# A fused loop over sequences: a written-out order for its head and its first two periods

## What is computed

```
h = silu(t @ sw1.T) * (t @ sw3.T)                  # shared expert of the first mixture
gate, xBC, dt = split(x @ W_in)
x, B, C = split(silu(conv4(xBC) + conv_b))
dt = softplus(dt + dt_bias); dA = exp(-exp(A_log) * dt)
h_t = h_(t-1) * dA_t + (dt_t * x_t) B_t;  y_t = h_t C_t + D_skip * x_t
y = rmsnorm(y * silu(gate)) * norm_w;     out = y @ W_out
w = top8(sigmoid(h @ gate_w)) normalised * 2.5     # second mixture
moe = shared(h) + sum_e w_e * (silu(h @ Wg_e) * (h @ Wu_e)) @ Wd_e
```

## Time and profile before

| | us |
|---|---|
| median of 3 runs | 1946.59 |
| lowest, highest | 1942.2, 1947.4 |
| the profiled execution | 1942.54 |
| its span (first to last instruction) | 1940.8 |
| TensorE busy | 1824.9 (94%) |
| VectorE busy | 1296.4 (67%) |
| ScalarE busy | 752.2 (39%) |
| GpSimd busy | 425.2 (22%) |
| mean granted clock of TensorE | 0.965 |

### The profile page before, as it was taken

How to read it: one execution, slowest core, us unless ns; L and a number is a source line. 1 busy time by engine, 2 the same in 40 slices (tenths; PEclk the granted TensorE clock), 3 DMA queues, 4 the chain that set the end, 5 groups by cost and what they waited for, 6 DMA issues and landing times.

```text
span 1940.8 us, 33575 instructions
## 1 busy us (share of the span) xinstructions
PE 1824.9 (94%) x9916; PEld 1406.5 (72%) x9917; DVE 1296.4 (67%) x3768; ACT 752.2 (39%) x1451; POOL 425.2 (22%) x708
## 2 busy tenths in 40 slices
...
DMA packets 92136, 137.88 MB, mean 71 GB/s; under 512 B 18564, under 2 KB 76164, under 8 KB 91524
## 3 DMA queue, kind: packets, MB, share of 16 engines
...
## 4 chain that ended last, share of the span: by engine, by line
PE 40%; issue 39%; DVE 11%; POOL 7%; ACT 2%; DMA 1%; DVEq 0%; POOLq 0%; SPq 0%; ACTq 0%
PE bank L610 6%; PE bank L184 5%; PE bank L631 4%; PE bank L1316 3%; POOL sorted_in L858 3%; PE bank L1274 2%; PE bank L193 2%; PE bank L1379 2%; PE bank L1322 2%; PE bank L1304 2%; PE bank L1407 2%; DVE tops L1560 1%; PE bank L621 1%; PE bank L539 1%; POOL down_w L2202 1%
## 5 line engine op out<-in xcount | busy, mean ns | idle before, releaser
L184 PE MATMUL bank<-moe_xT,up_w 128*128 128x256 f32 x2304 | 547.9, 381 | 0.0
L184 PEld LDWEIGHTS bank<-moe_xT,up_w 128*128 128x128 f32 x2304 | 439.8, 191 | 60.5 <-issue 0.2
L227 ACT ACTIVATE moe_silu<-bank 128x256 f32<-128x256 f32 x288 | 110.7, 384 | 574.6 <-PE bank L184 574.6
L193 PE MATMUL bank<-down_w,moe_hT 128*128 128x256 f32 x1152 | 304.0, 387 | 3.5 <-ACT moe_y L230 2.1
L193 PEld LDWEIGHTS bank<-down_w,moe_hT 128*128 128x128 f32 x1152 | 207.1, 190 | 37.0 <-issue 6.3
L1560 DVE TENSOR_REDUCE tops<-bank 128x4 f32<-128x1024 f32 (+1 forms) x96 | 117.4, 1223 | 54.7 <-PE bank L1316 52.9
L1461 ACT ACTIVATE probs<-bank 128x1024 f32<-128x1024 f32 x96 | 98.4, 1025 | 117.2 <-PE bank L1322 117.2
L830 DVE TENSOR_TENSOR moe_h<-moe_silu,bank 128x176 f32<-128x176 f32 x80 | 27.0, 338 | 138.7 <-issue 86.0
L610 PE MATMUL bank<-up_w,moe_xT 128*128 x320 | 115.5, 484 | 0.9 <-ACT moe_xT L676 0.6
L1316 PE MATMUL bank<-kT,qT 16*128 16x256 f32 (+1 forms) x1024 | 114.1, 351 | 0.0
L294 DVE TENSOR_TENSOR moe_hT<-moe_silu,bank 128x256 f32<-128x256 f32 x256 | 107.6, 420 | 8.8
...
...
## 6 DMA issues: line engine op xcount, KB each, us to landing
...
up_w<-in_up SPq DMA_DIRECT2D x2, 2304.0 KB, 12.6
```

Source lines behind the costliest of these rows:

```text
L184: last = mm(k.bank[:, UP_BANK + i % 3, half * S:(half + 1) * S], m.w_up[:, c, at + half * m.inter:at + (half + 1) * m.inter], m.xT[:, par, ...
L193: last = mm(k.bank[:, SUM_BANK, j * D:(j + 1) * D], m.hT[:, i % 3, j * P:(j + 1) * P], m.w_down[:, m.expert(i), :], start=(i == 0 and j == ...
L227: nc.scalar.activation(m.silu[:, i % 3, :], k.bank[:, UP_BANK + i % 3, 0:S], ACT.Silu).then_inc(m.silu_ready, 1)
```

## The change

- The order of the head is another one: the three `l_up` of `b` stand together behind `turn_dt` of sequence 0, and their silus are steps of their own (`l_silu`), behind the decay's transpose. `turn_dA`, `decay_out` and `decay_in` of sequence 0 stand ahead of its gates.
- Period 0 is the written-out list `FIRST`. The softplus and the decay of sequence 1 follow its `gating` 1 directly, its gates and convolution come behind, and `c_sum`, `c_norm`, `norm` and `turn_x` of sequence 2 are gone from it. At its end it has `up` 0 to 2, `h` 0 and 1 and `down` 0 of sequence 0, and `gmat` of sequence 1 ahead of `turn_c` of sequence 1.
- Period 1 is the written-out table `SECOND`, with 15 rounds (n = 3 to 17). The sum and norm of sequence 2 stand between the scans of sequence 1, the projections of sequence 2 two to four rounds later than before, and the sum and norm of sequence 3 at the end. Its rounds have `h` behind the other steps.
- The four products of `w_out` with `norm_w` on VectorE move from the start of the fused loop to the first mixture, ahead of its blocks.
- Waits of `m_turn`, `m_turn_c`, `turn_x` and `turn_c` are changed for the first sequences, to fit the bank's new order.

```diff
@@ moe_tensor
-            if not isinstance(t, int) or t + 1 < SEQS:
+            if isinstance(t, int) and t == 0:
+                pe.wait_ge(ssm.gate_ready, 4)
+            elif not isinstance(t, int) or t + 1 < SEQS:
                 pe.wait_ge(ssm.xtok_ready, 2 * t + 4)
...
-            if not isinstance(t, int) or t + 2 < SEQS:
+            if not isinstance(t, int) or 0 < t and t + 2 < SEQS:
                 pe.wait_ge(ssm.xT_ready, t + 3)
@@ sparse_vector
+    scale_w_out(k, m.ssm, dve)
     seen = [0]
@@ late_scalar
-        if what == "l_up":
+        if what == "l_silu":
@@ ssm_tensor
-            if begun(t - 1):
+            if isinstance(t, int) and t in (1, 2):
+                pe.wait_ge(m.xtok_ready, 2 * t)
+            elif begun(t - 1):
                 pe.wait_ge(moe.exp_ready, t - 1)
-            elif t == 1:
-                pe.wait_ge(m.xtok_ready, 2)
...
                 pe.wait_ge(m.gate_ready, 2 * t + 2)
+                if isinstance(t, int) and t == 1:
+                    pe.wait_ge(moe.combT_ready, 1)
@@
+def scale_w_out(k, m, dve):
+    dve.wait_ge(m.loaded, m.LOADS)
+    for f in range(FT):
+        last = k.nc.vector.tensor_scalar(m.w_out[:, f, :], m.w_out[:, f, :], m.norm_w[:, f:f + 1], None, ALU.mult)
+    last.then_inc(m.w_out_ready, 1)
@@ Tail
+    FIRST = (
+        ("gmat", 0, 0), ("scan", 0, 0), ("weight", 0, 0), ("c_fetch", 2, 0),
...
+        ("up", 0, 2), ("h", 0, 1), ("down", 0, 0), ("gmat", 1, 0), ("turn_c", 1, 0), ("turn_c", 1, 1),
+    )
+    SECOND = (
+        (("scan", 1, 0), ("weight", 1, 0), ("c_sum", 2, 0), ("xdt", 1, 0)),
...
+    )
@@ head
-        yield from self.period(0, 0)
-        yield "l_end", B, 0, 0
-        yield from self.period(1, 1)
+        for what, t, i in self.FIRST:
+            yield what, t, t % 2, i
+        for n, then in enumerate(self.SECOND, 3):
+            for what, t, i in (("up", 0, n), *then, ("h", 0, n - 1), ("down", 0, n - self.LAG)):
+                yield what, t, t % 2, i
```

More of the change, by code:

```diff
@@ L903, in sparse_sync @@
     go_through(m.blocks, sp, block)
-LATE_STEPS = ("l_norm", "l_turn", "l_up", "l_h", "l_down", "l_end")
+LATE_STEPS = ("l_norm", "l_turn", "l_up", "l_silu", "l_h", "l_down", "l_end")
 class Late:
```

44 lines of the change are left out of this document (33 added, 11 removed).

## The result

The changed kernel took 1952.49 us (median of 6 runs, 1949.52 to 1958.66) against 1946.25 before (6 runs) on the same chip in turns: a ratio of 1.0034, 95% interval 1.0019 to 1.005. It is slower by some 6 us. The forecast was 1947.0, which is 0.4 over the median then known, with a range of 1934.5 to 1957.0. The time is in the range, on the slow side, and 5.5 over the forecast.

What follows compares the result with a forecast made beforehand. Bound: TensorE in the hardware loop, before it a chain through VectorE, ScalarE and TensorE. First `up` +0.6 plus 1.9 for the clock gave +2.5: 1945.0 on the profiled execution, 1949.1 on the median, set at 1947; range 1934.5 to 1957.

Steps and rivals of the forecast that it cites:

- The start: Start of the fused loop: the four `w_out` products leave it and cost nothing in the first mixture, -1.2 us.
- The head: Steps up to `gating` 0: `turn_dt` spared two `l_up` (1.7), less waits; with a shorter decay DMA wait, -1.45 us in all.
- Period 0: Stretch from `gating` 1 to sequence 1's first scan: that scan starts at 881.2, 13.2 us ahead of 894.41.
- `turn_x`'s wait: Period 1: `turn_x` of sequence 2 waits for VectorE's `norm` 1, done at 903.8; TensorE idles 6 us ahead of it.
- `s_e` and the tables: Period 1: exp of sequence 2 at 931.1 holds VectorE; ScalarE's table loads (1.28 each) then hold `turn_c` 1 to 950.6.
- From `turn_c` 1 to the loop: End of period 1: 3.7 to `m_turn`, 2.5 copy and exp, 2.16 `m_route`, 1.1 the rest; first `up` at 960.1, +0.6.
- the clock's 1.9: One cost of TensorE's lower clock, 1.9 us, after the 6 us of idle ahead of `turn_x` of sequence 2.
- Base: Starting time: 1945.0 against the profiled execution, 1949.1 against the median of three runs; set between them at 1947.
- the fast one: Rival: period 1 after `turn_x` stays at TensorE's own work, early start kept; -9.8, or -7.9 with the clock; chance 0.27.
- The slow one: Rival: TensorE's lower clock holds from `m_turn` at 871.7 over the second mixture's entry; +8.8 in all; chance 0.22.

Runs made afterwards that it cites:

- e12: Changed kernel with the four products of `w_out` back at the start of the fused loop, timed again with more runs: 1954.49 us, ratio 1.0044 to before.
- e11: The changed kernel, unchanged, traced and timed a second time: 1952.89 us, ratio 1.0035 to the kernel before.
- e7: Changed kernel with the four products of `w_out` back at the start of the fused loop, first timing, four runs: 1957.57 us, ratio 1.0065 to before.
- e1: Changed kernel with the head's old order, periods 0 and 1 as changed: 1959.79 us, ratio 1.0063 to the kernel before.
- e9: Changed kernel with 25 unread products on TensorE ahead of `turn_x` of sequence 2, filling its wait: 1957.55 us, ratio 1.0061 to before.
- e4: Changed kernel with both softplus tables and `one_plus` of sequence 2 directly behind its `dt` 0: 1951.3 us, ratio 1.0025 to before.
- e3: Changed kernel with `norm` 1 of sequence 2 ahead of sequence 1's last scan, and `feat` of sequence 2 earlier: 1949.84 us, ratio 1.0021 to before.
- e8: The kernel before, unchanged, traced a second time: one run, 1949.73 us.
- e6: Changed kernel with sequence 2's `norm` 1 and `feat` earlier, decay's exp behind `turn_c`, and `bcdt` to `one_plus` ahead of `out`: 1943.85 us, ratio 0.9995 to before.

## Why the prediction was right and wrong

The forecast was +2.5 for the first `up` of the profiled execution and +0.4 for the time, with 43% for "no change"; what came is +5.3 there and 6 to 7 by the medians, "slower by over 0.3%", narrowly, which had 28%. The range held, and the mechanism is the predicted one: the early start is lost again to the waits of period 1. The sizes, step by step:

- **The start, -1.2: right.** `l_turn` starts at 800.32, which is 798.8 in the time of before, where it stood at 799.95; behind the products in the first mixture VectorE idles for 10.26 us, so they are hidden. e12 against e11 has them back at the same place, and its median is 1.6 higher.
- **The head, -1.45: the number was met by luck.** `c_sum` came 1.53 earlier than in the first trace of before, but only 0.19 earlier than in the second (37.77 for 37.96), and that although the products, 1.2, are gone. e7 and e12, one kernel, have it at 38.02 and 39.52: this point is known to 1.5 from one trace. The 1.7 that I took off for two `l_up` does not show in e1, which has the old head (37.25). What the head gains is 0.4 to 1.1 at `post` 0, and it is the wait for the decay's DMA, which I had at 0.35 and e1 has at 0.90.
- **Period 0, 13.2 us: right.** `post` 0 came at 863.8 in the time of before (forecast 865.2) and the first scan of sequence 1 at 880.5 (881.2): 13.9 earlier.
- **`turn_x`'s wait: right.** `norm` 1 of sequence 2 was done at 903.0 in the time of before (903.81 + 0.73 - 1.55), forecast 903.8; 5.82 of idle for the forecast 6. The lower clock behind it was put down as 1.9; against e9, which has full clock there, it is 2.4 in after and 1.6 in e11.
- **`s_e` and the tables: right.** `s_w` 137.3 relative, forecast 931.1 + 1.9, which is 137.4. `turn_c` 1 starts at 952.8 in the time of before, for the forecast 950.6 + 1.9 = 952.5. Four loads, each 1.28 to the next start and nothing on top: `s_e` starts 0.02 behind its load. The Trainium skill's rule (ScalarE: Activation LUTs, What ACT_TABLE_LOAD costs) of about 1380 ns of drain on top of each load is not borne out on this chain.
- **From `turn_c` 1 to the loop: undersized by 2.5, and this is the step that failed.** With the clock's 1.9 my sum had the first `up` at 962.0, 9.5 behind `turn_c` 1; it came at 964.9, 12.0 behind it (the other 0.3 is `turn_c` 1 itself). Two terms were missing. The lower clock came a second time, behind the 2.74 of idle ahead of `turn_c` 1: from there to the next `up` it took 2.98 (954.38 to 957.36) where e11 at full clock took 1.55, 1.4 more. I had put 0 to 3.8 beside the sum for such waits and nothing in it, as TensorE is not the bound there; behind this one it is. And `m_turn_c` starts at 965.32, 1.2 behind the last product of `m_route` (963.75 + 0.37), because it waits for sequence 3's `turn_x` and its copy (0.77 of idle in the row), which I had left out: only its own transpose and the `down` were in my list. The rest cancels: up to `m_turn` I had 3.7 for 3.3 at full clock, and 0.35 too little from there to the end of `m_route`. The first of the two terms is a matter of luck. Of eight traces with 2.7 to 3.1 of idle at this place, four pay it (after, e1, e4, e9) and four don't (e3, e7, e11, e12); e11, for one:
```profile
956.68 0.63 PE L1924 MATMUL bank<-ident,conv 128*128 128x128 f32 x4 [2.95 <-ACT down_w L2037]
```
- **Base: right by the trace, wrong by what the trace stood for.** I set +2.5 on a trace of before that lay 4.0 under the median, and took 2.1 off the 1949.1 that the median would have given. The trace's low total came from what lies ahead of the fused loop, which began at 795.6 (805.8 in e8); its fused loop was a slow one, 163.9 where e8 has 160.9. So against the middle of before the changed kernel loses some 1.5 more than against this trace, which a first trace can't tell, and the 2.1 should have stayed.

Of the rivals, the fast one did not come: `s_e` came at 932.7 in the time of before, far behind the 921 from which it decides. e6 meets its condition (`s_w` at 920.7), and there the first `up` is at 954.2, 5.3 ahead of before: part of the rival's 7.9. The slow one, a low clock over the entry of the second mixture, did not happen in after (`up` 0 1.97) but in part in e11 (two such rows, 1.12 for `m_turn` and 1.89 for the logits, and 3.50 for `up` 0; `gmat` 1.7 later). With the two missing terms the sum is 2.5 + 1.4 + 1.2 = +5.1, for the trace's +5.3.
